# Cross-attention prologue: box masks on 64 partitions right after the first split, special keys' products before tile 5, loads in another order, two score banks in batch -1

## The reference

```python
HEADS, NUM_IP_TOKENS, NUM_DUMMY_TOKENS, NEG = 20, 4, 4, -10000.0
q = _split_heads(hidden_states @ w_q, HEADS)
k = _split_heads(text @ w_k, HEADS)
v = _split_heads(text @ w_v, HEADS)
out_text = _merge_heads(_sdpa(q, k, v))
# mask_ip: for each box, 0 at grid points inside it and NEG outside;
# for the dummy keys NEG where any box covers the point, else 0
inside = (xg >= x1) & (xg <= x2) & (yg >= y1) & (yg <= y2)
ip_mask = jnp.where(inside, 0.0, NEG)
dummy = jnp.where(jnp.any(inside, axis=1), NEG, 0.0)
k_ip = _split_heads(ip_h @ w_k_ip, HEADS)
v_ip = _split_heads(ip_h @ w_v_ip, HEADS)
out_ip = _merge_heads(_sdpa(q, k_ip, v_ip, mask=mask_ip))
out = (out_text + out_ip) @ w_out + b_out + hidden_states
```

## Time and profile before

| | us |
|---|---|
| median of 3 runs | 549.91 (546.61 to 556.17) |
| profiled execution, whole | 547.39 |
| its span, first to last instruction | 545.6 |
| PE busy | 479.0 (88%) |
| DVE busy | 387.4 (71%) |
| ACT busy | 275.6 (51%) |
| POOL busy | 134.8 (25%) |
| PE's mean granted clock | 0.958 of full speed |

### The profile page before, as it was taken

One profiled execution on the slowest core, in us unless ns is written; L12 is line 12 of the kernel. 1 busy time (PEld: TensorE's weight loads), 2 busy tenths in 40 slices (PEclk: granted clock), 3 DMA queues, 4 the chain that ended last, 5 costly groups with the idle time before them and its releaser, 6 DMA issues.

```text
span 545.6 us, 11048 instructions
## 1 busy us (share of the span) xinstructions
PE 479.0 (88%) x4304; PEld 323.1 (59%) x4304; DVE 387.4 (71%) x706; ACT 275.6 (51%) x355; POOL 134.8 (25%) x206
## 2 busy tenths in 40 slices
PE   3969017799999999999999999999999999798895
PEld 2858016557666676667665766667566765455442
DVE  2733614868797778787797778777878779799832
ACT  3632001356665466545565565555664556566670
POOL 7013000004220313231422223130503131423441
PEclk9989658899999999999999999999999999999997
DMA  8988096485947777685859394948667565483011
GB/s 280 364 287 145 13 311 232 120 261 186 334 143 231 238 245 257 159 288 159 270 183 338 94 335 137 311 146 299 201 195 269 170 224 167 169 264 113 9 51 48
DMA packets 93956, 112.50 MB, mean 206 GB/s; under 512 B 14304, under 2 KB 72672, under 8 KB 93904
## 3 DMA queue, kind: packets, MB, share of 16 engines
q1 hardware_dynamic: 92960, 109.57, 62.5%
q0 software_dynamic: 944, 2.23, 2.4%
HBM read 73.17 MB, written 38.63 MB: 205 GB/s over the span
## 4 chain that ended last, share of the span: by engine, by line
issue 54%; POOL 21%; PE 9%; DMA 7%; DVE 6%; SPq 3%; ACT 1%; POOLq 0%; ACTq 0%; DVEq 0%
POOL o_turned L402 9%; POOL o_all L407 7%; POOL x_all L396 4%; DMA probs<-in_wv_ip 3%; DVE max_cols L558 2%; DMA v_rows<-v_out 1%; PE score_q L685 1%; PE score_q L645 1%; DMA q_stack<-aux_rows 1%; DVE x_all L514 1%; PE score_q L647 1%; PE score_q L646 1%; PE pj L757 1%; PE pv L748 1%; DMA raw<-in_xT 1%
## 5 line engine op out<-in xcount | busy, mean ns | idle before, releaser
L558 DVE TENSOR_REDUCE max_cols<-score_q 128x4 fp32r<-128x992 f32 x160 | 189.0, 1181 | 100.1 <-PE score_q L685 99.6
L483 ACT ACTIVATE probs<-score_t 128x1024 f32<-128x1024 f32 x160 | 163.4, 1021 | 142.4 <-PE score_t L734 142.3
L748 PE MATMUL pv<-probs,v_cur 128*32 128x256 f32 x1920 | 120.2, 383 | 0.6 <-ACT probs L483 0.6
L402 POOL TENSOR_TENSOR o_turned<-o_turned,inv_cols 128x256 f32<-128x256 f32 x80 | 53.9, 674 | 148.4 <-DVE inv_cols L601 148.2
L757 PE MATMUL pj<-wo_sb,o_all 128*128 128x320 f32 x192 | 70.6, 478 | 9.5 <-DVE out_sb L613 5.6
L748 PEld LDWEIGHTS pv<-probs,v_cur 128*32 128x32 f32 x1920 | 54.3, 109 | 39.0 <-issue 1.0
L396 POOL TENSOR_TENSOR x_all<-x_all,bias_sb 128x640 f32<-128x640 f32 x16 | 24.9, 1558 | 199.9 <-DMA x_all<-in_x 199.9
L685 PE MATMUL score_q<-k_stack,q_stack 64*128 64x256 f32 x440 | 46.3, 289 | 30.7 <-DMA q_stack<-aux_rows 23.1
L598 DVE STREAM_TRANSPOSE o_turned<-o_all 128x512 f32<-128x512 f32 x80 | 55.9, 699 | 11.8 <-ACT o_all L475 11.8
L734 PE MATMUL score_t<-q_stack,k_stack 64*128 64x256 f32 x440 | 55.5, 330 | 7.3 <-ACT probs L483 5.4
L475 ACT ACTIVATE o_all<-pv 128x512 f32<-128x512 f32 x80 | 47.8, 598 | 27.4 <-PE pv L748 27.4
(11 more groups left out here) (147 smaller groups left out, 635.5 us busy)
## 6 DMA issues: line engine op xcount, KB each, us to landing
k_stack<-k_parts SPq DMA_DIRECT2D x33, 320.0 KB, 5.1
q_stack<-q_parts SPq DMA_DIRECT2D x33, 320.0 KB, 6.7
v_rows<-v_out SPq DMA_DIRECT2D x32, 320.0 KB, 4.6
v_cur<-v_rows SPq DMA_DIRECT2D x16, 640.0 KB
q_parts<-qk_out SPq DMA_DIRECT2D x32, 256.0 KB, 3.2
k_parts<-qk_out SPq DMA_DIRECT2D x32, 248.0 KB, 6.2
raw<-in_ctxT SPq DMA_DIRECT2D x14, 512.0 KB, 5.1
x_all<-in_x SPq DMA_DIRECT2D x16, 320.0 KB, 7.5
```

The costliest lines, as they stand in the source:

```text
L402: pool.tensor_tensor(out, out, inv_cols[:, n % SLOTS, :].unsqueeze(2).broadcast_to([P, 2 * S // 32, DH]), ALU.mult).then_inc(scaled, 1)
L483: nc.scalar.activation(probs[:, slot(t % 2, p), :], score_t[:, :], ACT.Exp, scale=SCALE)\
L558: nc.vector.tensor_reduce(out=max_cols[:, h, :, at:at + 4:2].rearrange("p t e -> p e t"), in_=both[:, :, :, 0:TEXT], op=ALU.max, axis=AX.X ...
L748: last = mm(pv[32 * t:32 * t + 32, at:at + S], values_of(u, kind, 4 * k + t), probs[:, slot(u, 2 * k + t // 2), a:a + S], start=kind != 1, ...
```

## The change

Box masks: the host gives the boxes and the grid for 64 partitions (16 elements times 4 boxes), so five operations (`box_masks`) make all four box rows at once; a matmul of `inside` with a 64x16 matrix of ones (`box_sum`, sent behind the mask column) counts the boxes that cover a point, and one operation (`dummy_masks`) makes the dummy row. They stand around DVE's `tile(0)`, the matmul behind PE's `tile(0)`. POOL stores them in four DMAs.

Special keys: `special()` and its evacuations move from behind tile 9 (or 10) to behind tile 4.

Queues: SP loads `c` of group 1 after the store of tile 4, and `wo` and `bias` (`load_small`) after the store of tile 11; it waits for `ksp_stored` alone before the keys of the first stack, and for `aux_stored` before its queries. POOL loads the constant key rows after the masks are stored and `wvip` has landed.

Banks: in batch -1 the odd pairs use `score_t`, so PE may be a pair ahead of DVE; in return the first key scores wait for all ten maxima of element 0.

```diff
@@ -70,8 +70,8 @@
...
         v_out = sb("v_out", [P, 2, VW])
-        text_mask = sb("text_mask", [P, 1])
-        boxes = sb("boxes", [B, 16])
+        text_mask = sb("text_mask", [P, 1 + B])
+        boxes = sb("boxes", [B * NIP, 4])
         zeros = sb("zeros", [B, S])
@@ -102,30 +102,32 @@
...
         x_res = x_all[:, 0:2 * OT * D].rearrange("p (u t n) -> p u t n", u=2, t=OT)
-        parts = x_all[0:B, :].rearrange("p (k n) -> p k n", k=6)
-        grid_sb, inside, covered = parts[:, 0:2, :], parts[:, 2:5, :], parts[:, 5, :]
-        mask_out = v_cur[0:B, 0, 0:2, :].rearrange("p k n -> p (k n)").rearrange(
-            "p (j n) -> p j n", j=1 + NIP)
+        parts = x_all[0:B * NIP, :].rearrange("p (k n) -> p k n", k=6)
+        grid_sb, inside, box_mask, dummy_mask = parts[:, 0:2, :], parts[:, 2, :], parts[:, 3, :], parts[0:B, 4, :]
+        box_sum = text_mask[0:B * NIP, 1:1 + B]
         def bank(name, n):
...
         pj = bank("pj", 1)
-        def pair_at(b, p):
-            return 1024 * (p % 2) if b - 1 > LAST_HOST else 0
+        def double(b):
+            return b == 0 or b - 1 > LAST_HOST
+        def score_both(b, p):
+            if double(b) and p % 2:
+                return score_t[:, :] if b == 0 else score_q[:, 1024:2048]
+            return score_q[:, 0:1024]
         def score_bank(b, p, e):
-            at = pair_at(b, p) + 512 * e
-            return score_q[:, at:at + 512]
+            return score_both(b, p)[:, 512 * e:512 * e + 512]
         def score_pair(b, p):
-            at = pair_at(b, p)
-            return score_q[:, at:at + 1024].rearrange("p (e t n) -> p e t n", e=2, t=2)
+            return score_both(b, p).rearrange("p (e t n) -> p e t n", e=2, t=2)
         lone_banks = [pj[:, :], pv[:, :], score_t[:, 0:512], score_t[:, 512:1024], score_q[:, 1536:2048]]
...
         vsp_psum = score_q[:, 1024:1024 + D]
+        covered = score_q[0:B, 512 + P:512 + P + S]
         ld = {n: sem("loaded_" + n) for n in ("sp", "wkip", "wvip", "wq", "wk", "wv", "small", "boxes")}
@@ -143,6 +145,7 @@
...
         preset, mask_step, mask_done = sem("preset"), sem("mask_step"), sem("mask_done")
+        covered_ready = sem("covered_ready")
         kaux_stored, kaux_loaded = sem("kaux_stored"), sem("kaux_loaded")
@@ -263,8 +266,9 @@
...
             sp.dma_start(wvip_raw, rows(wv_ip)).then_inc(ld["wvip"], 16)
-            sp.dma_start(wo_sb[:, :, :], rows(wo)).then_inc(ld["small"], 16)
-            sp.dma_start(bias_sb[:, :], bias.broadcast_to([P, D])).then_inc(ld["small"], 16)
+            def load_small():
+                sp.dma_start(wo_sb[:, :, :], rows(wo)).then_inc(ld["small"], 16)
+                sp.dma_start(bias_sb[:, :], bias.broadcast_to([P, D])).then_inc(ld["small"], 16)
             def load_q(b, j):
@@ -298,16 +302,19 @@
...
                     store_tile(n)
+            lone(0, 5)
             for h in range(2):
                 load_c(1, h)
-            lone(0, 7)
+            lone(5, 7)
             load_x(1)
-            lone(7, 12)
+            lone(7, 10)
             sp.wait_ge(ksp_stored, 96)
+            load_stack_k(0)
+            sp.wait_ge(aux_stored, 96)
+            load_stack_q(0)
+            lone(10, 12)
             sp.wait_ge(sp_stored, 16)
-            sp.wait_ge(aux_stored, 64)
-            load_stack_k(0)
-            load_stack_q(0)
+            load_small()
             lone(12, 14)
@@ -368,16 +375,21 @@
...
                                ALU.mult).then_inc(preset, 1)
+            pool.wait_ge(w_low, 1)
+            pool.memset(halves(vsp_out)[1], 1.0).then_inc(preset, 1)
+            aux_of = aux_rows.rearrange("b (e r) n -> b e r n", e=2)
+            for e in range(2):
+                pool.dma_start(aux_of[:, e, MASKS:DH, :], zeros[:, :].unsqueeze(1).broadcast_to(
+                    [B, DH - MASKS, S])).then_inc(aux_stored, 16)
+            pool.wait_ge(mask_done, 1)
+            for e in range(2):
+                pool.dma_start(aux_of[:, e, 1:MASKS, :], box_mask).then_inc(aux_stored, 16)
+                pool.dma_start(aux_of[:, e, 0, :], dummy_mask).then_inc(aux_stored, 16)
+            pool.wait_ge(ld["wvip"], 16)
             pool.wait_ge(kaux_stored, 16)
...
                                kaux_rows.unsqueeze(1).broadcast_to([2 * DH, PAIRS, KEYS])).then_inc(kaux_loaded, 16)
-            aux_of = aux_rows.rearrange("b (e r) n -> b e r n", e=2)
-            for e in range(2):
-                pool.dma_start(aux_of[:, e, MASKS:DH, :], zeros[:, :].unsqueeze(1).broadcast_to(
-                    [B, DH - MASKS, S])).then_inc(aux_stored, 16)
-            pool.wait_ge(w_low, 1)
-            pool.memset(halves(vsp_out)[1], 1.0).then_inc(preset, 1)
             for m, r in enumerate(MT_ROWS):
@@ -387,9 +399,6 @@
...
             pool.dma_start(v_sp_rows.rearrange("b p n -> (b p) n"), vsp_out[:, :]).then_inc(sp_stored, 16)
-            pool.wait_ge(mask_done, 1)
-            for e in range(2):
-                pool.dma_start(aux_of[:, e, 0:MASKS, :], mask_out).then_inc(aux_stored, 16)
             def normalise(b):
@@ -453,17 +462,19 @@
...
             act.wait_ge(preset, 8)
-            for n in range(3, 7):
-                tile(n)
-            for h in range(2):
-                split_c(1, h)
-            for n in range(7, 10):
+            for n in range(3, 5):
                 tile(n)
...
             nc.scalar.activation(halves(vsp_out)[0], by_head(vsp_psum), ACT.Copy).then_inc(vsp_done, 1)
+            for n in range(5, 7):
+                tile(n)
+            for h in range(2):
+                split_c(1, h)
+            for n in range(7, 10):
+                tile(n)
             tile(10)
@@ -503,26 +514,19 @@
...
                 dve.wait_ge(mask_step, steps[0])
-            def mask():
+            def box_masks():
                 dve.wait_ge(ld["boxes"], 48)
                 gx, gy = grid_sb[:, 0, :], grid_sb[:, 1, :]
-                for j in range(NIP):
-                    side = lambda c: boxes[:, 4 * j + c:4 * j + c + 1]
-                    at = inside_j(j)
-                    then(nc.vector.tensor_scalar(at, gx, side(0), None, ALU.is_ge))
-                    for g, c, op in ((gx, 2, ALU.is_le), (gy, 1, ALU.is_ge), (gy, 3, ALU.is_le)):
-                        then(nc.vector.scalar_tensor_tensor(out=at, in0=g, scalar=side(c), in1=at,
-                                                            op0=op, op1=ALU.mult))
-                    then(nc.vector.tensor_scalar(mask_out[:, 1 + j, :], at, -NEG / SCALE, NEG / SCALE,
-                                                 ALU.mult, ALU.add))
-                    if j == 0:
-                        then(nc.vector.tensor_copy(covered, at))
-                    else:
-                        then(nc.vector.tensor_tensor(covered, covered, at, ALU.max))
-                nc.vector.tensor_scalar(mask_out[:, 0, :], covered, NEG / SCALE, None, ALU.mult)\
+                side = lambda c: boxes[:, c:c + 1]
+                then(nc.vector.tensor_scalar(inside, gx, side(0), None, ALU.is_ge))
+                for g, c, op in ((gx, 2, ALU.is_le), (gy, 1, ALU.is_ge), (gy, 3, ALU.is_le)):
+                    then(nc.vector.scalar_tensor_tensor(out=inside, in0=g, scalar=side(c), in1=inside,
+                                                        op0=op, op1=ALU.mult))
+                then(nc.vector.tensor_scalar(box_mask, inside, -NEG / SCALE, NEG / SCALE, ALU.mult, ALU.add))
+            def dummy_masks():
+                dve.wait_ge(covered_ready, 1)
+                nc.vector.tensor_scalar(dummy_mask, covered, 1.0, NEG / SCALE, ALU.min, ALU.mult)\
                     .then_inc(mask_done, 1)
-            def inside_j(j):
-                return inside[:, j % 3, :]
             n_low = [0]
@@ -568,7 +572,9 @@
...
                 split_c(0, h)
+            box_masks()
             tile(0)
+            dummy_masks()
             split_x(0)
@@ -577,19 +583,18 @@
...
             low(wvip_hl[:, 1], wvip_raw, wvip_hl[:, 0])
+            for m, r in enumerate(MT_ROWS):
+                dve.wait_ge(ksp_hi, m + 1)
+                nc.vector.tensor_tensor(ksp_parts[0:r, 1, m, :], ksp_out[m][0:r, :],
+                                        ksp_parts[0:r, 0, m, :].bitcast(f32), ALU.subtract).then_inc(ksp_lo, 1)
             for h in range(2):
...
                 tile(n)
-            for m, r in enumerate(MT_ROWS):
-                dve.wait_ge(ksp_hi, m + 1)
-                nc.vector.tensor_tensor(ksp_parts[0:r, 1, m, :], ksp_out[m][0:r, :],
-                                        ksp_parts[0:r, 0, m, :].bitcast(f32), ALU.subtract).then_inc(ksp_lo, 1)
             tile(10)
...
             tile(12)
-            mask()
             dve.wait_ge(preset, 8)
@@ -673,10 +678,13 @@
...
                         pe.wait_ge(kaux_loaded, 48)
-                if pair_at(b, 1) == 0 or p == 0:
+                if p == 0 or not double(b):
                     need(pe, max_done, n)
...
```

(22 more changed lines are left out.)

## The result

The changed kernel takes 524.18 us by the median of 4 runs (522.69 to 526.6), the kernel before 551.22 (4 runs, 546.61 to 556.17). The ratio is 0.954, 95% interval 0.9461 to 0.9619: faster by 4.6%. The profiled execution took 523.65 us with a span of 521.8; PE's mean granted clock is 0.984, where it was 0.958. The forecast was 519 in a range of 508 to 531, and 518.4 for the profiled execution. The medians lie 27.0 us apart, the profiled executions (547.39 and 523.65) only 23.7, because the profiled execution of before lies 3.8 us under its median. Where in the kernel that difference arises no profile shows.

The account below looks back on a forecast made before the run. PE was taken as the bound from batch 0 on, with mask, mask store and stack load in a row behind PE in the prologue. Gains of 23 and 6 us gave 547.4 - 29 = 518.4 us profiled; point 519, range 508 to 531.

Parts of the forecast that it names:

- The place of the gain: Prologue and batch -1: batch 0 starts at 75.5 us in place of 104.6, what follows moving as a block; chance 0.60.
- loss at `wkip`'s low part: PE's `special()` behind tile 4: waits for this part, done at 23.3 us, while tile 4 ends near 23.1; 0.2 us lost.
- context landed: Group 1's context in the prologue: loaded from 24.5 us on, a landing up to 34.5 costs nothing.
- stack loads start: SP in the prologue: loads of the first stack start at 41 us instead of 67.37, behind query and special-key stores.
- my middle value: Batch -1: 20.5 us, taken between 16.6 and the 26.3 of before; gain 6 us.
- The sum of 16.6: DVE in batch -1: 16.6 us as the bound, from first scores, ten maxima, two low parts, one split and one turn.
- PE's sum: PE in batch -1: ten times four score products and five tiles of 1.8 us at full clock, 14 us.
- From there to the end 441 us as before: From the first key scores of batch 0 to the end: 441 us, as before the change.
- case E: Batch 0's first waits hold the shifted prologue for another 20 us, time 539 and more; chance 0.04.
- rival C: DMA bounds the prologue: first stack at 62 us, batch -1 keeps 24, time 528 to 531; chance 0.18.
- B: Engines alone bound the prologue, DMA hidden: batch -1 starts at 51 us, time 510 to 513; chance 0.15.
- D: Slower: PE waits behind tile 0 for `mask_step`, so a late grid stops everything; time above 550 us; chance 0.03.

Follow-up runs that it names:

- e6: Changed kernel with the load of group 2's second context half in its own buffer, issued behind `store_rows(0, 0)` without waiting for `split_c(2, 0)`: median 523.74 us.
- e10: Changed kernel with the special keys' small pieces stored in two parts, elements 0 to 3 at once, the rest after element 0's maxima: median 523.79 us.
- e11: Changed kernel with e6, e9 and e10 put together: median 521.30 us over 6 runs, ratio to before 0.9448.
- e5: Changed kernel with the load of group 2's second context half issued ahead of `load_rows(0, 0)` in batch -1: median 524.13 us.
- e8: e6 with `wo` and `bias` also loaded behind `load_rows(0, 0)`: median 524.02 us.
- e12: Changed kernel with 24 unused 512-column products on PE between tile 14 and the first scores: median 527.66 us.
- e9: Changed kernel with `store_rows(0, 0)` issued ahead of the second stack's queries, `load_stack_q(1)`, in batch -1: median 524.57 us.
- e7: Changed kernel with the special keys' small pieces stored a second time, into a scratch tensor, the stack waiting for all twelve stores: median 534.01 us.
- e1: Changed kernel with batch -1 back on one pair of score banks, without the first key scores' wait on the ten maxima: median 530.86 us.

## Why the prediction was right, and by how much it was off

**The place of the gain: right.** Batch 0 was forecast at 75.5 and starts at 75.19. That it is met within 0.3 us is luck: the stack loads started 3.9 us late, the stack took 2.4 us less than allowed, and batch -1 was 1.8 us shorter than the value chosen. The prediction's steps and what they measured:

| step | forecast | measured |
|---|---|---|
| box masks on DVE | 2.1 us, done at 12.7 | 2.2 us, done at 13.4 |
| boxes and grid later | at most 1 us | 0.8 us (9.46 for 8.65) |
| counting matmul | 0.4 us | 0.6 us (and the clock rose 1.3 us later in tile 0: tile 1 starts 1.2 us later in all) |
| loss at `wkip`'s low part | 0.2 us | 0.36 us |
| end of lone tiles | 50.3 | 50.6 |
| context landed | by 34.5 for free | 35.1, PE not held |
| query stores issued | by 40.5 | by 44.7 |
| stack loads start | 41 | 44.90 |
| first scores | 55 | 56.51 |
| batch -1 | 20.5 us | 18.7 us |
| first keys | 75.5 | 75.19 |
| from there to the end | 441.0 us | 446.6 us |
| profiled execution | 518.4 | 523.65 |

**Sizes off inside the prologue.** SP's issues were put at the lengths that they had before. The three loads of `x` took 6.5 us to issue where they took 1.6 before. DMA is at 1.08 from 30 to 40 us, where it was at 0.75 before; the query stores ended 4.2 us late:

```profile
34.20 1.69 SPq L224 DMA_DIRECT2D o_all<-in_xT  x1
35.93 4.78 SPq L226 DMA_DIRECT2D o_all<-in_xT  x2
40.76 3.97 SPq L242 DMA_DIRECT2D q_parts<-qk_out  x6
44.90 1.97 SPq L280 DMA_DIRECT2D k_stack<-k_parts  x3
```

The stack itself then came 11.6 us after its first issue, where 14 had been allowed, so the start was off by 1.5 only. Batch -1 was shorter than my middle value by 1.8 us; DMA did fill it, as feared, but what waited was not batch -1. One reading behind that step was wrong: of DVE's 24.8 us of waiting for PE, 15.4 are a single wait that begins before the first scores, so in the batch of 26.3 us DVE stood some 10. The sum of 16.6 does not use it. And PE's sum was taken at full clock: its products, 14 us there, took 16.1 at 0.88, and 19.3 before at 0.77.

**The step that was off: the last one.** "From there to the end 441 us as before" was 446.6; this one term, 5.6 us, with -0.3 for batch 0's start, is the whole difference of 5.3 us. I had case E, a loss in batch 0's first waits, at 20 us or nothing and gave it 0.04. It happened at a quarter of that size, and a longer last stretch is among the signs by which the prediction called itself wrong: of this one term it was. The prediction said that `store_rows` and `load_rows` queue behind the second stack, and priced that in batch -1; it did not follow SP's order one entry further, to the load of group 2's context behind `load_rows`, nor see that ACT has the first exponential behind the split of that context. e6 showed that this wait is real (3.92 us, 0.94 without it) and that removing it wins 1.4 us at the third keys, since the rows came later and the clock was lower. By the medians the gain was 27.0 us of the 29 forecast; the 5.6 us are measured between the two profiled executions.

**Part of rival C was right.** The first stack is what PE waits for at the end of the prologue, with DMA at 0.92 and more up to there; it came at 56.5 and not at 62. B (engines alone) was out: it would have needed first scores at 51. Of e10 and e11, which get them to 53.0 and 52.5, e10 loses nearly all of it again, while e11 is still 4.2 us ahead at the third keys. D did not happen (the masks had 1.4 us to spare).

**The low clock** is the second part of the loss. Tile 20, twelve products from 82.26 to 86.5, ran partly at the lower level (0.51 from 80 to 85), 4.2 us where a key tile takes 2.8 at full clock (tiles 10 to 14 took 12.0 us, less two value tiles of 1.8, over three). With the score products beside it that makes the 1.8 us of the 5.7 found above. It follows on 75 to 80 us, where PE was busy for 0.89 us of 5. In e5, e6 and e8 to e12 PE's products in the same stretch took 7.1 to 8.2 us, 2.4 to 3.5 over the 4.67 of before, which is part of why removing waits gave so little. These prices are read from rows; no experiment changed the clock there by itself.

## What to carry to other kernels

When a chain of small serial steps stands alone in a trace, moving it into holes of the same engine can be worth its whole length, down to the next limit (the masks alone: 14 us at the first scores, 9.4 at the third keys); so add up the transfers of the shortened stretch, not only the engines, before taking the engines' sum. Where the last forecast step is "from here on as before", walk the in-order queue and each engine's program two or three entries past that point: a transfer that was idle-time work before is now in a queue of its own making. In a stretch with DMA above 0.9, reordering transfers (e5, e9, e10) gave little here; whether fewer or larger pieces would give more was not tried. When a wait is taken out of one engine, look at the other terms of the same stretch too: here part of each gain went into PE's lower clock. And price a queue by the time its packets took, not by how much later the kernel got when they were doubled.

## What the runs showed of the hardware that I had not expected

Issuing is not a fixed cost: two loads that took 1.16 us of SP's time before took 4.78 with DMA at 1.08, and POOL stood 11.2 us ahead of one issue in e7. Writes of 32-byte pieces took as much DMA time for 0.33 MB (3.9 us) as 1.3 MB do at 341 GB/s. A DMA of 32 KB, the rows' store, took 2.4 us before, 5.6 with DMA above 1.0 at its issue, and 7.6 in e10. And a second pair of banks raised PE's mean clock in batch -1 from 0.68 (e1) to 0.88, worth more than the waits for DVE that it removed.
